# A twelve-stage decoder on one core: layer norm scales of twelve tiles made beside the last pair of the stage ahead

## What is computed

```python
def _layernorm(x, axis=-1, eps=1e-05):
    m = jnp.mean(x, axis=axis, keepdims=True)
    v = jnp.var(x, axis=axis, keepdims=True)
    return (x - m) / jnp.sqrt(v + eps)
```

## Time and profile before

| | |
|---|---|
| median of 3 runs | 1889.66 us (1888.14 to 1890.19) |
| the profiled execution | 1893.76 us, span 1891.9 us |
| PE busy | 1442.2 us, 76% of the span |
| DVE busy | 1222.2 us, 65% |
| ACT busy | 920.1 us, 49% |
| POOL busy | 337.8 us, 18% |
| mean granted clock of PE | 0.868 |

### The profile page before, as it was taken

How to read it: one execution, slowest core, us unless ns; L and a number is a source line. 1 busy time by engine, 2 the same in 40 slices (tenths; PEclk the granted TensorE clock), 3 DMA queues, 4 the chain that set the end, 5 groups by cost and what they waited for, 6 DMA issues and landing times. The chain is left out here.

```text
span 1891.9 us, 32347 instructions
## 1 busy us (share of the span) xinstructions
PE 1442.2 (76%) x11270; PEld 878.7 (46%) x11270; DVE 1222.2 (65%) x4051; ACT 920.1 (49%) x1998; POOL 337.8 (18%) x358
## 2 busy tenths in 40 slices
PE   5998878862875679994555699999983995778864
PEld 2554434441763534441233356666652883544432
DVE  7776468855336777776666477777665224667876
ACT  4554256641222345553622277777761442146656
POOL 3320012111534144300021000000002333312100
PEclk9999889985997889996577599999995997689995
DMA  3320014211561024310010000000003571004300
GB/s 123 55 50 2 1 17 57 35 34 40 153 141 31 12 56 62 58 18 19 0 58 1 12 7 7 7 7 12 2 3 103 176 204 58 23 17 60 43 2 22
DMA packets 60159, 84.53 MB, mean 45 GB/s; under 512 B 8352, under 2 KB 46496, under 8 KB 59488
## 3 DMA queue, kind: packets, MB, share of 16 engines
q1 hardware_dynamic: 55008, 72.24, 16.0%
q0 software_dynamic: 4992, 10.23, 2.8%
HBM read 51.18 MB, written 9.18 MB: 32 GB/s over the span
## 5 line engine op out<-in xcount | busy, mean ns | idle before, releaser
L638 DVE TENSOR_REDUCE maxs<-ps 128x4 f32<-128x1024 f32 x192 | 234.9, 1224 | 62.5 <-PE ps L966 60.9
L794 ACT ACTIVATE L_xattn_probs<-ps 128x1024 f32<-128x1024 f32 x192 | 196.5, 1024 | 85.3 <-PE ps L991 80.9
L3385 ACT ACTIVATE wide_pr<-wide_sc,wide_nm 128x256 f32<-128x256 f32 x256 | 127.0, 497 | 13.0 <-DVE wide_nm L3320 12.4
L1478 POOL DMA_INDIRECT moe_xs<-normed,moe_table x92 | 87.0, 946 | 162.9 <-DVE moe_table L1445 73.2
L966 PE MATMUL ps<-keys,L_xattn_qs 64*128 64x256 bf16 x768 | 75.3, 274 | 38.2 <-DVE maxs L638 31.9
L1007 PE MATMUL ps<-L_xattn_probs,values 128*32 128x256 f32 x1536 | 102.8, 385 | 0.0
L3292 DVE CUSTOM_DVE_ANT_0 wide_sc<-ps,wide_mask 128x256 f32<-128x256 f32 x256 | 93.8, 420 | 10.3 <-PE ps L3410 9.3
L3315 DVE COPY wide_prT<-ps 128x512 f32<-128x512 f32 x64 | 44.3, 692 | 81.4 <-PE ps L3423 81.2
L1885 DVE SCALAR_TENSOR_TENSOR moe_z_sb<-ps,moe_wt,moe_a_sb 128x256 f32<-128x256 f32 x46 | 22.3, 484 | 92.1 <-ACT moe_a_sb L1917 77.4
L991 PE MATMUL ps<-L_xattn_qm,keys 64*128 64x256 bf16 x768 | 74.6, 272 | 7.3 <-ACT L_xattn_probs L794 7.0
L3330 DVE TENSOR_SCALAR wide_pr<-wide_pr,wide_inv 128x256 f32<-128x256 f32 x256 | 75.6, 349 | 1.8
(11 more groups left out here) (636 smaller groups left out, 3697.7 us busy)
## 6 DMA issues: line engine op xcount, KB each, us to landing
moe_wt<-in_packed_experts SPq DMA_DIRECT2D x23, 707.0 KB
moe_wt<-in_packed_experts SPq DMA_DIRECT2D x23, 384.0 KB
keys<-L_xattn_k_parts SPq DMA_DIRECT2D x108, 64.0 KB
L_xattn_qs<-L_xattn_q_parts SPq DMA_DIRECT2D x108, 64.0 KB
expert_out<-moe_y SPq DMA_DIRECT2D x46, 128.0 KB
weights<-in_packed_L_xattn SPq DMA_DIRECT2D x2, 1316.0 KB, 7.4
keys<-L_attn_k_parts SPq DMA_DIRECT2D x36, 64.0 KB
L_attn_qs<-L_attn_q_parts SPq DMA_DIRECT2D x36, 64.0 KB
```

What stands on the lines that cost most here:

```text
L638: v.tensor_reduce(nm, ps[:, BANK_M:BANK_M + 2, :].rearrange("p j (t n) -> p j t n", t=2), AX.X, ALU.max, negate=True).then_inc(S("m_used"), 1)
L794: a.activation(probs[:, s % RING, :, :, :].rearrange("p j t n -> p j (t n)"), ps[:, BANK_P:BANK_P + 2, :], ACT.Exp, scale=HD ** -0.5)\
L1478: g.indirect_dma_start(self.xs[:, j % BUFS, h * P:(h + 1) * P], None, C.normed, bass.IndirectOffsetOnAxis(self.table[:, n:n + 1], 0))\
L3385: ins = a.activation(pr[:, s % 3, j, qt, :], sc[:, s % 2, j, qt, :], ACT.Exp, bias=nm[:, s % 2, n:n + 1], accum_out=sums[:, s % 2, n:n + 1])
```

## The change

A helper makes scale and shift of tiles 0 to 11 as a generator (36 steps; two more with the mean square). Each stage but 2 and 8 hands it to its own loop as `beside`, and the stage behind takes the flag `normed_ahead` and leaves its first norm out; it makes the norm of tiles 12 to 15 itself. In `attend8` and `wide_attention` the generator is begun at s = SLOTS in the place of `side`.

```diff
+AHEAD = 3 * PT
+def norm_steps(v, L, C, a, b, rows=None, mean_square=False, done=None):
+    x = C.x if rows is None else rows
...
+    for t in range(a, b):
+        yield L.tick(v.bn_stats(C.stats[:, t, :], x[:, t * D:(t + 1) * D]))
+    L.settle()
+    for t in range(a, b):
+        yield L.tick(v.bn_aggr(C.mv[:, t, :], C.stats[:, t, :]))
+    L.settle()
+    if mean_square:
+        yield L(v.tensor_tensor(mean, mean, mean, ALU.mult))
+        yield L(v.tensor_tensor(var, var, mean, ALU.add))
+    yield L(v.tensor_scalar(nv, var, LN_EPS, None, ALU.add))
+    yield L(v.tensor_scalar(root.bitcast(I32), nv.bitcast(I32), -0.5, 1597463007.0, ALU.mult, ALU.add))
+    for _ in range(3):
+        yield L(v.scalar_tensor_tensor(na, root, -0.5, root, ALU.mult, ALU.mult))
+        yield L(v.tensor_tensor(na, na, nv, ALU.mult))
+        yield L(v.scalar_tensor_tensor(root, na, 1.5, root, ALU.add, ALU.mult))
+    if not mean_square:
+        ins = v.scalar_tensor_tensor(C.shift[:, a:b], mean, -1.0, root, ALU.mult, ALU.mult)
...
+def norms_for_next(v, L, C, added, n, **kind):
+    C.normed_ahead = True
+    v.wait_ge(added, n)
+    yield from norm_steps(v, L, C, 0, AHEAD, **kind)
+def beside_last(steps, phases, lag, t):
+    if t >= phases + 2 * lag:
+        for _ in range(-(-40 // lag)):
+            next(steps, None)
```

In `weave` and `weave_ahead`:

```diff
                 next(unit, None)
+        beside_last(beside, phases, lag, t)
+    drain(beside)
```

At the end of the slots (`attend8`; `wide_attention` likewise, with `AHEAD // 2` sequences added):

```diff
+                    if s == SLOTS:
+                        side = norms_for_next(v, L, C, S("added"), PAIRS - 1, rows=inner, mean_square=rope)
```

The start of a cross attention, DVE, ACT and PE:

```diff
-                for _ in norms(0, PT):
-                    pass
+                if rope:
+                    drain(norms(0, PT))
+                elif not normed:
+                    drain(norms(0, AHEAD))
...
-                if not rope:
-                    values(0)
...
                 split_query()
-                for _ in second_pair:
-                    pass
+                if rope:
+                    drain(second_pair)
+                else:
+                    values(0)
...
+                    for t in range(PT):
+                        centre(0, t, 0, xn[:, t, :], "xn_ready")
                     whole(0, 1)
                     first(0, 1)
-                    for t in range(PT):
-                        centre(0, t, 0, xn[:, t, :], "xn_ready")
                     turned_in(0)
...
                     project(0, BANK_B, "wk", kvT(0), "k_proj")
-                    project_values(0, FIRST_V, range(PT))
                     turn_normed(0)
                     if boundary is not None:
                         count_ends()
                     pe.wait_ge(S("hT_ready"), 1)
                     project(0, BANK_A, "wq", hT[:, :], "q_proj")
+                    project_values(0, FIRST_V, range(PT))
```

The routers, DVE, ACT and PE:

```diff
+    even(0, AHEAD)
+    drain(norm_steps(v, L, C, AHEAD, TILES, done=C.sem("rstd_ready")))
+    even(AHEAD, TILES)
...
+    centre_odd(a, C, xn, range(1, AHEAD, 2), normed)
+    for m in range(PAIRS - 1):
+        copy_turned(a, C, hT, m)
+    centre_odd(a, C, xn, range(AHEAD + 1, TILES, 2), normed)
+    copy_turned(a, C, hT, PAIRS - 1)
...
+    for m in range(PAIRS - 1):
+        turned(m)
+    pe.wait_ge(C.weights_loaded[k], 32)
+    for m in range(PAIRS - 1):
+        logits(m)
+    turned(PAIRS - 1)
+    logits(PAIRS - 1)
```

The bit FFN (DVE), and a table of ACT's that is loaded at its start:

```diff
-                    if m == 0:
-                        norm_columns(v, L, C, 0, PT)
+                    if m == 0 and not normed:
+                        drain(norm_steps(v, L, C, 0, AHEAD))
...
                     if m == 0:
                         quantise_weights()
-                        norm_columns(v, L, C, PT, TILES)
                     yield
...
                     yield
+                    if m == 0:
+                        drain(norm_steps(v, L, C, AHEAD, TILES))
                     yield
...
+                a.preload_act_table_set("silu_and_others")
```

More of the change, by code:

```diff
@@ L121, in take_tail, with take_normed @@
         return tail
+    def take_normed(self):
+        normed, self.normed_ahead = self.normed_ahead, False
+        return normed
     def region(self, k):
@@ L323, in attend8 @@
     KINDS = 2 if rope else 1
-    normed = lambda m: min(m, 2) + 1
+    normed = C.take_normed()
+    after = (lambda m: min(m, 2) + 1) if rope else (lambda m: (not normed) + (m == PAIRS - 1))
     with ExitStack() as ctx:
@@ L557, in norms @@
                 def norms(a, b):
+                    if not rope:
+                        yield from norm_steps(v, L, C, a, b, done=S("rstd_ready"))
+                        return
                     n = b - a
@@ L1242, in pair @@
                     v.tensor_tensor(xs, xs, ps[:, B + 1, :], ALU.add).then_inc(S("added"), 1)
-                weave([pair(m) for m in range(PAIRS)], PHASES, LAG)
+                weave([pair(m) for m in range(PAIRS)], PHASES, LAG,
+                      beside=norms_for_next(v, L, C, sem(2)("added"), 1))
                 v.wait_ge(sem(PAIRS - 1)("added"), 1)
@@ L2135, in _ @@
                 fronts = [tail.front(v, L, m) if tail else iter(()) for m in range(PAIRS)]
-                weave_ahead(fronts, PT + 1, [pair(m) for m in range(PAIRS)], PHASES, LAG)
+                weave_ahead(fronts, PT + 1, [pair(m) for m in range(PAIRS)], PHASES, LAG,
+                      beside=norms_for_next(v, L, C, sem(2)("added"), 1))
                 v.wait_ge(sem(PAIRS - 1)("added"), 1)
```

208 lines of the change are left out of this document (96 added, 112 removed).

## The result

The changed kernel takes **1866.44 us** in the median (four runs, 1865.88 to 1868.47) against 1889.11 us: a ratio of 0.9882, 95% interval 0.9865 to 0.9899: 22.7 us, 1.2% faster. The forecast was 1866, 23 us. The profiled execution took 1868.47 us. So the total was met. The question of this study is whether its terms were, and part of them were not: errors of 2 to 5 us in single stages cancelled.

What follows compares the result with a forecast made beforehand. No engine is full; chains of waits at stage barriers bind. Start gains of 37.45 us less tail costs of 14.5 make 23 us, 1870.8 against the profiled execution, so 1866 for the median; range 1857 to 1877.

Steps and rivals of the forecast that it cites:

- Tails: Ten stage ends: norm steps for the next stage laid ahead of the barrier cost 14.5 us in all, bounds 12 and 18.
- Starts: Stage starts: norms removed there gain 37.45 us in all, each worth what the next releaser allows.
- my pair: Stage 8's router start: gain 6.2 us at full clock or 2.95 us at half clock.
- one of my signs of being wrong: Routers of stages 2 and 8: another granted clock over them would show the prediction wrong; no size given.
- the middle value of 4.6: Stage 8's router start: gain taken as 4.6 us, between the half-clock 2.95 and the full-clock 6.2.
- I take 1.5, 1.7 and 1.3 for the three; bounds 0.2 and 2.3 each: Starts of the three cross attentions (stages 1, 4, 10): gains in us; key placing begins only 0.4 us earlier.
- My rival on the clock: Routers and cross starts: PE stays at 2.4 GHz, 7.7 us more, 31 us in all, 1859; chance 0.20.
- from there its token tiles take 2.6 us: ReLU attention's start: after POOL's bias split at 964.3, token tiles end at 966.95, before 971.48; gain 4.5 us.
- The port rule: ReLU attention's start: DVE and GpSimd lock each other out of shared ports, delaying biases; gain about 3 us, not 4.5.
- a slot with such steps is at most 0.1 us longer: Wide attention's stream: four later norms go, worth only 0.25 us, beside 0.8 us at its start.
- the fourth rival: All starts: the flag never reaches the next stage, twelve tiles are made again and tails paid; near 1912; chance 0.02.
- Starts give less: Cross starts nothing of 4.5, ReLU 3, stage 8 2.95, a tail or two worse by 1; net about 14, 1875; chance 0.17.

Runs made afterwards that it cites:

- the kernel with the bit FFN's late tail: Changed kernel with all 36 of the bit FFN's ahead-steps done in DVE's wait behind the last pair's second half: 1865.56 us, ratio 0.9845.
- the late wait: Changed kernel with each small norm step waited for only ahead of the next small step, not right behind itself: 1869.97 us, ratio 0.9874.
- the kernel with wasted tails: Changed kernel with the norm steps made in the tails but thrown away, each start making twelve tiles again: 1913.29 us, ratio 1.0118.
- the kernel with three edits: Changed kernel plus ReLU's first bias signalled early, wide's steps ahead of its last addition, bit's steps in its last wait: 1861.51 us, ratio 0.9809.
- the three and the four together: Changed kernel with ReLU-bias, wide-tail and bit-tail edits: 1861.51 us (0.9809); also waiting for small norm steps only ahead of the next: 1859.20 us (0.9798).

## Why the prediction was right, point by point

**Tails.** The rule that I used (steps before the last addition are free up to DVE's wait, steps behind it cost all, steps between two instructions of the chain cost all) held where the half clock was alike within 1.1 us: SwiGLU, bit, wide and stage 4 together 9.0 us measured, 9.5 forecast. Block was mis-sized: sixteen steps into a wait of 1.38 cost 1.1 us and not 2.25. The order of steps inside wide is as said: 13 behind the addition; the four that stand between the normalisations made PE's turning late by 0.63 us (bounds 0.6 and 1.4, taken 0.95).

**Starts.** SwiGLU, bit and stage 2's router came out within 0.5 us of their steps. In stage 8 the logits were read 2.9 us sooner, which is the half-clock end of my pair (2.95), and the granted clock was 0.50 over them, before 0.93, one of my signs of being wrong; the middle value of 4.6 was the error there, and the stage kept 2.0. In the int8 FFN the row maximum came 4.3 us sooner into the stage (3.85 predicted); the 0.7 us beyond that went with half clock of 34 us in place of 42 to 44.

**Stage 10: the step that failed** is "I take 1.5, 1.7 and 1.3 for the three; bounds 0.2 and 2.3 each", with what the first slots were to give. Key placing, which I had put 0.4 us sooner, starts 8.7 us into stage 1 (before 10.0) and 7.3 into stage 10 (before 8.9):

```profile
254.29 3.04 PE L1105 MATMUL ps<-L_xattn_k_parts,lay 128*128 128x512 bf16 x12
...
1667.97 2.77 PE L1105 MATMUL ps<-L_xattn_k_parts,lay 128*128 128x512 bf16 x12 [0.72 <-POOL L_xattn_k_parts L543]
```

In stage 4 it is not sooner: 9.3 us into the stage, before 8.4 and 9.4. That was one of my own signs of being wrong, and yet this stage gained 2.2 us where I had 1.9; by which path is not shown. In stage 10 the gain is 3.4 us at the first maximum, 1.7 by the fall of the clock that went, and 1.4 at the first slots of the second pair, where I had 0.4 (every changed kernel shows 1.2 to 1.6 there; why is open). Without the 1.7 of the clock's earlier rise the start gives 1.7, within my bounds. So about 3.4 of the 5.1 us beyond the forecast are the clock's (an estimate from these three profiles), and what I missed is that the clock is part of this start. My rival on the clock named the cross starts, but gave each 1 us more.

**ReLU attention: the step that failed** is "from there its token tiles take 2.6 us". That duration was from a stretch at 2.4 GHz. In all three profiles of the changed kernel they started at 1.2 GHz and their first pair took 1.48 to 1.49 us, not 0.81: DVE's `lin_k_rot`, which waits for them, started 17.7, 17.1 and 14.7 us into the stage (before 17.7). In the one profile of this code in which they ran at 2.4 GHz, that of the kernel with the bit FFN's late tail, it started at 13.2 and the stage took 97.6 us, where the forecast makes 97.2 (101.4 - 4.2). So the term was right at one clock and taken for both. The wait for POOL's split, 2.25 to 2.81 us, is real: without it the stage is shorter in every profile, by 1.6 us at least. The port rule that I had weighed against this start is borne out in part. POOL's first cast took 0.50 us before and 1.60 in the first profile after, beside DVE's table products (0.67 in all other profiles with norms made ahead), and single DVE steps beside POOL's subtractions took 0.77 in place of 0.16 us, as some did before (POOL before, then POOL and DVE after):

```profile
957.13 0.50 POOL L259 CAST lin_kkv_parts<-weights 96x384 bf16<-96x384 f32 x1
```

```profile
940.59 1.60 POOL L320 CAST lin_kkv_parts<-weights 96x384 bf16<-96x384 f32 x1
...
943.78 0.92 POOL L323 TENSOR_TENSOR lin_kkv_rest<-lin_kkv_rest,lin_kkv_middle 96x384 f32<-96x384 f32 x1
```

```profile
943.76 0.16 DVE L215 SCALAR_TENSOR_TENSOR newton_a<-rstd 128x4 f32<-128x4 f32 x1
943.95 0.77 DVE L216 TENSOR_TENSOR newton_a<-newton_a,newton_v 128x4 f32<-128x4 f32 x1
```

POOL's last memset ended 9.47 us into the stage in the first profile and 8.9 in the two others, before 8.70. The Trainium skill's page "SBUF — State Buffer" (SBUF: two separate sides) says that the two engines lock each other out of a shared port pair for a whole instruction; the rows agree. But its price, 0.2 to 0.8 us of POOL, was the small part.

**Wide: the step that failed** is "a slot with such steps is at most 0.1 us longer". It came from rows of the old generator. The removed norms gave 0.07 each, as said, and the start 0.46 (0.8). The two norms that stayed, now made by the new helper, cost 1.07 each, because each small step's wait stands ahead of the next instruction of the stream; the late wait took them away. The table shows only +3.3 us against 2.5 because the second profile before had 32 us of half clock in this stage; against the first, which had 26 us like the changed kernel, it is +4.6, and the 2.1 us over the forecast are these two norms. I had read the helper and counted its instructions, not its waits.

**The sum.** Stage 10 gained 5.1 us more than forecast, block 2.1, int8 1.1, six others 1.5 together. ReLU fell 3.9 short, stage 8 2.6, wide 0.8, and stage 0, whose start the change does not touch, was 1.2 longer. The errors sum to -1.3 us (-24.3 against -23.0) in the means of the profiles. One sum of the prediction is wrong in itself: the fourth rival's terms, 14.5, 2 at each of seven starts, less 3, make +25.5 and 1915, not 1912; the kernel with wasted tails came out at +25.5. So the total was right through cancelling, not through the precision of its terms, and the range of 20 us was an honest width for it. "Starts give less" and "the clock stays up" each happened, in different stages: stage 8's logits and ReLU's tiles ran at half clock, stage 10's start at full.

**What stays open.** Why the clock rises after 11.8 us in one profile of ReLU attention and after 29 in another of the same kernel isn't settled, nor why stage 0 takes 175.0 or 177.5 us; the profiles of 177.4 to 177.6 us have half clock for 3.4 us from 17 us into that stage and again over its last 6 to 7 us, those of 175.0 have at most 1.2 us of it at the end. The Trainium skill's page "TensorE: Matmul & The Clock Gate" (What's actually happening) says that the point of the rise varies from one run of a kernel to the next. The repeats agree with that in ReLU attention. Stage 10 shows it more rarely: its clock rose at 4 us, and it took 157.9, in all three profiles of the changed kernel and in three more with an edit elsewhere, but rose at 9.9 us in the kernel with three edits. Which of these parts of stage 10's gain comes from the order of work and which from the norm is not separated. And each of the edits alone is shown by its stage's length; in the totals only the three and the four together stand clear of the changed kernel.

## What to carry to other kernels

Cost a start at both clock levels: the same start of stage 10 gave 1.7 us at one and 3.4 at the other, and ReLU's token products took 1.49 or 0.81 us a pair. Look for every operand that PE's first long run of matmuls waits for: bringing the first one sooner is worth little while a second one (here a bias that POOL splits) still comes late. In a generator that runs beside a stream, place each wait right ahead of the step that needs it; a wait issued behind a step is paid by whatever comes next. Put steps for the next stage into the one long wait ahead of the last result, none between the instructions of the last chain and none behind it.

## What was not expected of the hardware

A stage of one unchanged program differed by up to 3.6 us (ReLU attention 99.0 to 102.6, half clock for 61.5 to 71.9 us of it), and flow attention by 2.9 (112.2 to 115.1); yet other stages repeat to 0.1 us. A first rise of the clock 5.8 us later cost stage 10 1.8 us. One wait on DVE's own semaphore between small steps and 256-column instructions cost 0.13 us each (0.46 against 0.33 between normalisations). And the kernel before had medians of 1887.8 to 1898.5 us in the three groups, so that edits of 2 to 3 us could be told only by stage.
